# Moving the probabilities-times-V product to the end of each attention window in a two-layer transformer kernel

## Chip, core and metric

One core of a Trainium2 chip runs the whole kernel. The metric is the device time in microseconds (us). Five engines work side by side, each through its own list of instructions in order: TensorE (PE in the rows; PEld is its weight load), VectorE (DVE), ScalarE (ACT), GpSimd (POOL) and SyncE (SP, which here only issues DMAs). They meet through semaphores.

## What is computed

Two transformer layers on 2 x 512 tokens of width 256, all in float32. The part that matters here is the second attention, with 16 heads of width 128, causal:

```python
x = x + L0_attn(layernorm(x))      # 3 heads of width 256
x = x + L0_ffn(layernorm(x))       # ternary weights, 256 -> 1024 -> 256
# second attention, on layernorm(x):
q = x @ W_Q + b_Q;  k = x @ W_K + b_K;  v = x @ W_V + b_V     # 16 heads
scores = where(causal, q @ k.T / sqrt(128), -100000)
z = softmax(scores) @ v
x = x + z @ W_O + b_O
x = x + int8_linear(layernorm(x))
```

## The kernel before

Every matmul in higher precision is done three times, on operands split into a high and a low part (`split_mm`, lines 266 to 270: high times high, and the two mixed products). So each result of a matmul is read twice from its PSUM bank: ACT writes the rounded part (`..._hi`), and then DVE writes what is left (`..._lo`).

The first layer's attention is folded: a matrix GF = Wq.T Wk for each of 3 heads (uses 0 to 2 of the loop at lines 322 to 337) and Wv.T fcT (uses 3 to 5). The loads for it are issued by SP (lines 278 to 291) and ACT (lines 622 to 627). The first layer norm stands in the middle of this loop on PE (`layernorm_turn(0)` before use 2, line 326) and its vector part ahead of all on DVE (line 955).

The second attention runs in 32 windows, w = 4p + ww: p is the pair of heads (8 pairs, whose weights are loaded together into the tile `stage`), and the four windows of a pair are 2 batches x 2 heads. The last windows overlap the next pair: the loop runs `window(p, ww)` for ww = 1 to 4, after a single `window(0, 0)`. Each engine goes through a window by an order written out by hand (lines 211 to 222), with one letter and a number for each step:

- T0 to T3: the normalised probabilities PR of token block 0 to 3 of this window are transposed on PE (`turn`, 10 transposes in all), split by ACT (PT_hi, `probs_hi`) and DVE (PT_lo, `probs_lo`).
- A0: probabilities times V on PE (`attend`, 12 matmuls); on ACT and DVE A0 is the split of its result Z (`z_high`, `z_low`).
- O0, O1: Z times W_O on PE (`project_out`), and on DVE its sum into X (`add_out`). They stand in even windows alone. O0 in the window ww = 2 needs the Z of the window before it.
- S0 to S3: scores of the **next** window on PE (`scores`), the masked maximum on DVE (`max1`), the exponential on ACT (`exp1`). S3 on PE must not start before DVE has taken the maximum of S1, since both use bank 3 (line 501).
- Q0, K1, V2: projections for the window after the next, split by ACT and DVE. W2 on ACT and DVE is the split of the V2 that PE ended the window before with.
- B0 is, in the two last windows, the split of the Z of the window before.

`recip1` on DVE inverts the sums of the exponentials (part 0 for blocks 0 to 2, part 1 for block 3), POOL then multiplies PR by them (`normalise`), and T0 to T3 of the next window wait for that (line 512). Per pair, `load_a` (parts 0, 1, 2 for the weights of Q, K, V, on DVE) and `split_a` (POOL) split the new weights in windows ww = 1 and 2, `load_b` and `split_b` those of W_O in ww = 4.

## Time and profile before

| | |
|---|---|
| time of the kernel, median of 3 runs | 552.83 us (551.98 to 553.96) |
| the profiled execution's own time | 551.98 us |
| its span in the trace | 550.1 us |
| PE busy | 523.9 us, 95% of the span |
| DVE, ACT, POOL busy | 71%, 50%, 35% |
| one pair in the steady state (four windows) | 43.35 us |

The span is the stretch that the trace covers; 1.9 us of the time lie around it. Rows of a timeline are: start in us from the span's start, duration in us, engine, line of the kernel, operation, output tile <- input tiles, partitions x elements, number of instructions merged into the row, and in square brackets the idle time before it with what ended it. Durations of instructions that follow each other on an engine overlap a little (by 0.05 to 0.1 us), so what one costs its engine is the distance of the starts. Times on PE are distances of starts too, since its ends are modelled. Rows of a table of stretches give the stretch and its length, then the busy us and number of instructions of PE, PEld, DVE, ACT and POOL, the granted clock of PE as a share of 2.4 GHz, the DMA share and GB/s.

### The profile page before, as it was taken

How to read it: one execution, taken by the hardware profiler on the slowest of the kernel's cores; microseconds unless marked ns; L12 is line 12 of the kernel's file. 1: busy time of each engine (PE TensorE's matmuls, PEld its weight loads, DVE VectorE, ACT ScalarE, POOL GpSimd, SP SyncE). 2: the span in 40 equal slices, each digit the busy share in tenths (PEclk: the TensorE clock that was granted, in tenths of full speed). 3: DMA queues.
4: the chain of work that ended last, by engine and by line, in shares of the span. 5: the costliest groups of instructions: out<-in, count | busy, mean ns of one | idle time of the engine just before them, and what ended most of it. 6: DMA issues, size and time to landing. Idle time of an engine off the chain costs nothing.

```text
span 550.1 us, 9165 instructions
## 1 busy us (share of the span) xinstructions
PE 523.9 (95%) x3280; PEld 465.2 (85%) x3280; DVE 393.0 (71%) x992; ACT 277.5 (50%) x671; POOL 191.3 (35%) x274
## 2 busy tenths in 40 slices
...
GB/s 269 352 1 1 1 1 1 2 0 1 2 1 1 1 78 1 1 78 1 1 78 1 1 38 42 1 1 78 1 2 78 1 1 77 2 1 0 2 0 77
DMA packets 8316, 17.52 MB, mean 32 GB/s; under 512 B 464, under 2 KB 6736, under 8 KB 7248
## 3 DMA queue, kind: packets, MB, share of 16 engines
...
q8 instruction: 27, 0.44, 0.3%
...
HBM read 15.88 MB, written 1.05 MB: 31 GB/s over the span
## 4 chain that ended last, share of the span: by engine, by line
PE 67%; DVE 15%; ACT 8%; issue 5%; DMA 2%; POOL 1%; SPq 0%; DVEq 0%; ACTq 0%
PE bank L268 16%; PE bank L270 16%; PE bank L269 16%; ACT PR L721 5%; PE bank L515 4%; DVE SM L1212 3%; PE bank L442 3%; PE bank L441 3%; DMA fcT_sb<-fcT 2%; PE bank L507 2%; PE bank L505 2%; PE bank L506 2%; ACT K_hi L716 2%; PE bank L452 1%; PE bank L454 1%
## 5 line engine op out<-in xcount | busy, mean ns | idle before, releaser
L721 ACT ACTIVATE PR<-SM,nmax 128x128 f32<-128x128 f32 (+3 forms) x128 | 71.8, 562 | 120.1 <-DVE nmax L1212 120.1
L870 POOL TENSOR_TENSOR PR<-PR,rec 128x128 f32<-128x128 f32 x32 | 12.8, 400 | 151.0 <-DVE rec L1219 151.0
L1212 DVE CUSTOM_DVE_ANT_0 SM<-bank,causal 128x128 f32<-128x128 f32 (+3 forms) x128 | 60.2, 480 | 0.0
L1223 DVE TENSOR_TENSOR PT_lo<-bank,PT_hi 128x128 fp32r<-128x128 f32 (+3 forms) x128 | 59.5, 487 | 0.5 <-ACT PT_hi L726 0.3
L832 POOL TENSOR_TENSOR E_lo<-E,E_hi 128x512 fp32r<-128x512 f32 x24 | 31.1, 1301 | 57.7 <-DVE E_hi L1024 50.7
L515 PE MATMUL bank<-ident,PR 128*128 128x128 f32 x320 | 48.1, 276 | 3.2 <-POOL PR L879 1.1
L268 PE MATMUL bank<-XT_hi,W_hi 128*128 128x512 f32 x128 | 50.6, 396 | 0.1
L270 PE MATMUL bank<-XT_hi,W_lo 128*128 128x512 f32 x128 | 50.6, 395 | 0.0
L269 PE MATMUL bank<-XT_lo,W_hi 128*128 128x512 f32 x128 | 50.5, 394 | 0.0
L726 ACT CAST PT_hi<-bank 128x128 fp32r<-128x128 f32 (+3 forms) x128 | 48.6, 420 | 1.2 <-PE bank L515 1.0
L505 PE MATMUL bank<-K_hi,Q_hi 128*128 128x256 f32 (+2 forms) x128 | 46.6, 364 | 0.0
L268 PE MATMUL bank<-PT_hi,V_hi 128*128 128x256 f32 (+2 forms) x128 | 43.4, 339 | 1.4 <-DVE PT_lo L1223 1.4
L515 PEld LDWEIGHTS bank<-ident,PR 128*128 128x128 f32 x320 | 36.3, 140 | 9.8 <-POOL PR L879 3.6
L1202 DVE SCALAR_TENSOR_TENSOR Q_lo<-bank,bqk,Q_hi 128x512 fp32r<-128x512 f32 x32 | 24.0, 750 | 28.4 <-ACT Q_hi L716 28.4
L270 PE MATMUL bank<-PT_hi,V_lo 128*128 128x256 f32 (+2 forms) x128 | 42.2, 330 | 0.0
L269 PE MATMUL bank<-PT_lo,V_hi 128*128 128x256 f32 (+2 forms) x128 | 42.1, 329 | 0.0
L507 PE MATMUL bank<-K_hi,Q_lo 128*128 128x256 f32 (+2 forms) x128 | 41.6, 325 | 0.0
L506 PE MATMUL bank<-K_lo,Q_hi 128*128 128x256 f32 (+2 forms) x128 | 41.4, 324 | 0.0
L655 ACT ACTIVATE E<-bank,nmax 128x512 f32<-128x512 f32 x24 | 16.5, 689 | 48.8 <-DVE nmax L1018 48.8
L268 PE MATMUL bank<-WO_hi,Z_hi 128*128 128x256 f32 x128 | 36.7, 287 | 1.8 <-DVE Z_lo L1229 1.8
L1229 DVE SCALAR_TENSOR_TENSOR Z_lo<-bank,bv,Z_hi 128x512 fp32r<-128x512 f32 x32 | 23.9, 747 | 18.6 <-ACT Z_hi L731 17.9
L1219 DVE RECIPROCAL rec<-sum 128x3 f32<-128x3 f32 x64 | 10.7, 168 | 36.7 <-ACT PR L721 36.7
...
## 6 DMA issues: line engine op xcount, KB each, us to landing
...
wraw<-wgateT SPq DMA_DIRECT2D x1, 1024.0 KB, 12.8
...
```

Of the source, the lines that this page charges most:

```text
L268: pe.matmul(dst, a_hi, b_hi, start=first, stop=False, skip_group_check=share)
L269: pe.matmul(dst, a_hi, b_lo, start=False, stop=False, skip_group_check=share)
L270: return pe.matmul(dst, a_lo, b_hi, start=False, stop=last, skip_group_check=share)
L505: pe.matmul(dst[:, 0:n], Q_hi[:, slot, cols], K_hi[:, slot, 0:n], start=True, stop=False)
L506: pe.matmul(dst[:, 0:n], Q_hi[:, slot, cols], K_lo[:, slot, 0:n], start=False, stop=False)
L507: pe.matmul(dst[:, 0:n], Q_lo[:, slot, cols], K_hi[:, slot, 0:n], start=False, stop=True).then_inc(s_psum, 1)
L515: mm = pe.transpose(bank[4 + c % 2][:, j * P:(j + 1) * P], PR[:, c, j * P:(j + 1) * P], ident[:])
L721: act.activation(PR[:, c, 0:(c + 1) * P], SM[:, c % 2, 0:(c + 1) * P], ACT.Exp, bias=nmax1[:, c:c + 1], scale=-1.0, accum_out=sum1[:, c:c ...
L726: act.copy(PT_hi[:, 0:c + 1, c * P:(c + 1) * P], bank[4 + c % 2][:, 0:(c + 1) * P].rearrange("p (j q) -> p j q", q=P)).then_inc(pt_hi, 1)
L832: pool.tensor_tensor(E0_lo[:, m, :], E0[:, m, :], E0_hi[:, m, :], ALU.subtract).then_inc(e0_lo, 1)
L1212: dve.tensor_tensor_reduce(SM[:, c % 2, 0:n], bank[2 + c % 2][:, 0:n], causal[:, SEQ - n:SEQ], 1.0, HIGHEST, ALU.add, ALU.min, nmax1[:, c: ...
L1223: dve.tensor_tensor(PT_lo[:, 0:c + 1, c * P:(c + 1) * P], bank[4 + c % 2][:, 0:(c + 1) * P].rearrange("p (j q) -> p j q", q=P), PT_hi[:, 0 ...
```

## The change

**Orders of the windows.** On PE, A0 moves from the middle to the very end of each window, and Q0 stands in third place in even windows too. On ACT and DVE the split of Z is taken out of the window and stands as B0 in the next one: first of all on ACT, and on DVE behind T1 and ahead of S0. The split of V2 moves the other way, from the next window (W2) into its own (V2). `recip1` gets a letter of its own (R0, R1), R1 behind V2. On DVE `load_a` part 0 moves ahead of S2, part 1 to the end of window 1, part 2 to the start of window 2. POOL's `split_a`, `split_b` move to fit.

```diff
-        EVEN_PE = steps("T0 T1 S0 O0 T2 T3 S1 Q0 S2 O1 A0 K1 S3 V2")
-        EVEN_ACT = steps("T0 T1 W2 O0 S0 T2 T3 S1 Q0 S2 O1 A0 K1 S3")
-        EVEN_DVE = steps("T0 T1 S0 W2 O0 T2 T3 S1 Q0 S2 O1 A0 K1 S3")
-        ODD_PE = steps("T0 T1 S0 Q0 T2 T3 S1 S2 K1 A0 S3 V2")
-        ODD_ACT = steps("T0 T1 W2 S0 Q0 T2 T3 S1 S2 K1 A0 S3")
-        ODD_DVE = steps("T0 T1 S0 W2 Q0 T2 T3 S1 S2 K1 A0 S3")
+        EVEN_PE = steps("T0 T1 S0 Q0 O0 T2 T3 S1 S2 K1 O1 S3 V2 A0")
+        EVEN_ACT = steps("B0 T0 T1 W2 S0 Q0 T2 T3 S1 S2 K1 S3 V2")
+        EVEN_DVE = steps("T0 T1 B0 S0 W2 Q0 O0 T2 T3 S1 S2 K1 R0 O1 S3 V2 R1")
+        ODD_PE = steps("T0 T1 S0 Q0 T2 T3 S1 S2 K1 S3 V2 A0")
+        ODD_ACT = steps("B0 T0 T1 S0 Q0 T2 T3 S1 S2 K1 S3 V2")
+        ODD_DVE = steps("T0 T1 B0 S0 Q0 T2 T3 S1 S2 K1 R0 S3 V2 R1")
-        LAST = {"pe": (steps("T0 T1 S0 S1 O0 T2 T3 S2 O1 S3 A0"), steps("T0 T1 T2 T3 A0")),
-                "act": (steps("T0 T1 W2 S0 S1 T2 T3 S2 S3"), steps("T0 T1 T2 T3 B0 A0")),
-                "dve": (steps("T0 T1 S0 S1 W2 O0 T2 T3 S2 O1 S3"), steps("T0 T1 T2 T3 B0 A0"))}
+        LAST = {"pe": (steps("T0 T1 S0 S1 T2 T3 O0 S2 S3 O1 A0"), steps("T0 T1 T2 T3 A0")),
+                "act": (steps("B0 T0 T1 S0 S1 T2 T3 S2 S3"), steps("B0 T0 T1 T2 T3 A0")),
+                "dve": (steps("T0 T1 B0 S0 S1 T2 T3 O0 S2 R0 S3 O1 R1"), steps("T0 T1 B0 T2 T3 A0"))}
...
-                if first and kind == "O":
+                if first and kind in "OB" or kind == "W" and not first:
...
             def window(p, ww, first=False, last=False):
                 w = 4 * p + ww
+                if ww == 2 and not last:
+                    dve.wait_ge(pj_lo, 12 * p + 12)
+                    load_a(p + 1, 2)
...
-                        if c == CT - 2 and ww == 1 and not last:
+                        if c == 1 and ww == 1 and not last:
                             dve.wait_ge(pj_lo, 12 * p + 10)
                             load_a(p + 1, 0)
...
+                if ww == 1 and not last:
+                    dve.wait_ge(pj_lo, 12 * p + 11)
+                    load_a(p + 1, 1)
```

**Start.** The loads are issued in the order Wk (3), X of batch 0, Wv by head (3, was one), X of batch 1, the three biases, the int8 weights; fcT goes to ACT's queue. Eight matmuls on a tile of ones run on PE before the first load has landed. The first layer norm moves behind uses 3 and 4 on PE, and into the loop on DVE; the vector part of the second one (`ln_normalise(1)`) moves behind the first split of Y.

```diff
+            for _ in range(WARM):
+                pe.matmul(bank[0][:, 0:P], ones[:], ones[:], start=True, stop=True)
             for g in range(GF_USES):
                 h = g % H0
-                pe.wait_ge(*((ld_qk0[h], 32) if g < H0 else (ld_v0, 32)))
-                if g == 2:
+                if g < H0:
+                    pe.wait_ge(ld_qk0[h], 32)
+                else:
+                    pe.wait_ge(ld_v0[h], 16)
+                    pe.wait_ge(ld_fc, 16)
+                if g == H0 + 2:
+                    pe.wait_ge(consts, 1)
                     layernorm_turn(0)
...
             y_low(0)
+            ln_normalise(1)
```

On PE, in an odd window, from the first row of K1 (the projection of K, twice three matmuls) on. Before, `PT_hi,V_hi` (A0) stands between K1 and the last scores:

```order
L268 MATMUL bank<-XT_hi,W_hi 128x512 [waits pj_lo]
...
L270 MATMUL bank<-XT_hi,W_lo 128x512
L268 MATMUL bank<-PT_hi,V_hi 128x512 [waits z_free,t_free]
L269 MATMUL bank<-PT_lo,V_hi 128x512
...
L505 MATMUL bank<-K_hi,Q_hi 128x512 [waits s_max]
L506 MATMUL bank<-K_lo,Q_hi 128x512
```

The changed kernel at the same place, where S3 (`K_hi,Q_hi` of 512 columns, which waits for a maximum) is next to K1, and A0 follows V2 (`W_hi,XT_hi`):

```order
L271 MATMUL bank<-XT_hi,W_hi 128x512 [waits pj_lo]
...
L273 MATMUL bank<-XT_hi,W_lo 128x512
L518 MATMUL bank<-K_hi,Q_hi 128x512 [waits s_max]
L519 MATMUL bank<-K_lo,Q_hi 128x512
L520 MATMUL bank<-K_hi,Q_lo 128x512
L271 MATMUL bank<-W_hi,XT_hi 128x256 [waits pj_lo]
...
L271 MATMUL bank<-PT_hi,V_hi 128x512 [waits z_free,t_free]
```

So the last scores come one A0 earlier behind K1. On DVE, the end of window ww = 1 and the start of ww = 2. Before (`W_hi<-stage` is `load_a`, `SM,nmax` is `max1`):

```order
L1139 CAST W_hi<-stage 128x512 [waits pj_lo]
L1140 COPY bqk<-stage 128x2
L1229 SCALAR_TENSOR_TENSOR Z_lo<-bank,bv,Z_hi 128x512 [waits z_hi]
L1212 ISA SM,nmax<-bank,causal 128x512 [waits s_exp,s_psum,masks]
L1212 ISA nmax 128x1
L1219 RECIPROCAL rec<-sum 128x1 [waits s_exp]
L1223 TENSOR_TENSOR PT_lo<-bank,PT_hi 128x128 [waits pt_hi]
L1223 TENSOR_TENSOR PT_lo<-bank,PT_hi 128x2x128 [waits pt_hi]
L1212 ISA SM,nmax<-bank,causal 128x128 [waits s_exp,s_psum,masks]
```

The changed kernel on DVE at the same place:

```order
L1219 ISA SM,nmax<-bank,causal 128x512 [waits s_exp,s_psum,masks]
L1219 ISA nmax 128x1
L1206 TENSOR_TENSOR V_lo<-bank,V_hi 128x512 [waits pj_hi]
L1226 RECIPROCAL rec<-sum 128x1 [waits s_exp]
L1146 CAST W_hi<-stage 128x512 [waits pj_lo]
L1147 COPY bqk<-stage 128x2
L1149 CAST W_hi<-stage 128x512 [waits pj_lo]
L1230 TENSOR_TENSOR PT_lo<-bank,PT_hi 128x128 [waits pt_hi]
L1230 TENSOR_TENSOR PT_lo<-bank,PT_hi 128x2x128 [waits pt_hi]
L1236 SCALAR_TENSOR_TENSOR Z_lo<-bank,bv,Z_hi 128x512 [waits z_hi]
L1219 ISA SM,nmax<-bank,causal 128x128 [waits s_exp,s_psum,masks]
```

Between the last maximum and the first PT_lo there now stand V_lo and two loads of weights, and Z_lo has come between PT_lo and the first maximum of the window.

## Rows read from the trace of the kernel before

**Rows 1.** Page, its head: the span and busy time of each engine.

```profile
span 550.1 us, 9165 instructions
PE 523.9 (95%) x3280; PEld 465.2 (85%) x3280; DVE 393.0 (71%) x992; ACT 277.5 (50%) x671; POOL 191.3 (35%) x274
```

**Rows 2.** Windows ww = 1 to 4: stretch, length, then busy us and instructions.

```profile
241.32:250.58 9.26, 9.26 (x61) 8.26 (x59) 7.59 (x23) 6.12 (x16) 2.76 (x6) 1.00 0.34 114
250.58:263.26 12.68, 12.48 (x84) 11.25 (x83) 8.73 (x23) 6.45 (x16) 4.58 (x7) 1.00 0.00 0
263.26:272.58 9.32, 9.32 (x60) 8.23 (x59) 6.64 (x19) 6.12 (x16) 2.39 (x5) 1.00 0.01 2
272.58:284.67 12.09, 12.09 (x85) 11.26 (x84) 8.13 (x23) 6.51 (x16) 3.64 (x6) 1.00 0.01 1
```

**Rows 3.** Timeline, PE, window ww = 3: its T0, T2, A0 and S3.

```profile
263.26 0.49 PE L515 MATMUL bank<-ident,PR 128*128 128x128 f32 x3
...
265.36 0.94 PE L515 MATMUL bank<-ident,PR 128*128 128x128 f32 x7
...
268.43 0.50 PE L268 MATMUL bank<-PT_hi,V_hi 128*128 128x512 f32 x1
...
270.46 0.39 PE L505 MATMUL bank<-K_hi,Q_hi 128*128 128x512 f32 x1
```

**Rows 4.** Timeline, DVE, the same window: T0 and T1, S0, Q0, T2 and T3, S1, A0.

```profile
264.52 0.70 DVE L1223 TENSOR_TENSOR PT_lo<-bank,PT_hi 128x128 fp32r<-128x128 f32 x2
265.14 0.28 DVE L1212 CUSTOM_DVE_ANT_0 SM<-bank,causal 128x128 f32<-128x128 f32 x1
...
266.57 0.75 DVE L1202 SCALAR_TENSOR_TENSOR Q_lo<-bank,bqk,Q_hi 128x512 fp32r<-128x512 f32 x1 [0.53 <-ACT Q_hi L716]
267.23 1.14 DVE L1223 TENSOR_TENSOR PT_lo<-bank,PT_hi 128x384 fp32r<-128x384 f32 x2
268.30 0.41 DVE L1212 CUSTOM_DVE_ANT_0 SM<-bank,causal 128x256 f32<-128x256 f32 x1
...
271.39 0.75 DVE L1229 SCALAR_TENSOR_TENSOR Z_lo<-bank,bv,Z_hi 128x512 fp32r<-128x512 f32 x1
272.05 0.68 DVE L1212 CUSTOM_DVE_ANT_0 SM<-bank,causal 128x512 f32<-128x512 f32 x1
```

**Rows 5.** Timeline, ACT: Z of one window, then S3, T0 and T1, Q0.

```profile
259.94 0.69 ACT L731 ACTIVATE Z_hi<-bank,bv 128x512 fp32r<-128x512 f32 x1 [0.41 <-PE bank L270]
...
263.53 0.72 ACT L721 ACTIVATE PR<-SM,nmax 128x512 f32<-128x512 f32 x1 [1.43 <-DVE nmax L1212]
...
264.25 0.52 ACT L726 CAST PT_hi<-bank 128x128 fp32r<-128x128 f32 x2
...
265.86 0.67 ACT L716 ACTIVATE Q_hi<-bank,bqk 128x512 fp32r<-128x512 f32 x1
```

**Rows 6.** Timeline, DVE, the last step of window ww = 1.

```profile
252.33 0.17 DVE L1219 RECIPROCAL rec<-sum 128x1 f32<-128x1 f32 x1 [0.88 <-ACT PR L721]
```

**Rows 7.** Timeline, DVE, window ww = 1: the splits of the new weights.

```profile
247.10 0.42 DVE L1134 TENSOR_SCALAR W_hi<-stage 128x512 fp32r<-128x512 f32 x1
...
247.56 0.69 DVE L1137 SCALAR_TENSOR_TENSOR W_lo<-stage,W_hi 128x512 fp32r<-128x512 f32 x1
...
249.34 0.78 DVE L1139 CAST W_hi<-stage 128x512 fp32r<-128x512 f32 x1
```

**Rows 8.** Timeline of the start: GF uses 0 and 1, uses 3 to 5, second layer norm.

```profile
4.91 6.56 PE L336 MATMUL bank<-Wk_sb,Wq_sb 128*128 128x256 f32 x16 [4.91 <-DMA Wk_sb<-wk]
...
15.87 5.45 PE L336 MATMUL bank<-fcT_sb,Wv_sb 128*128 128x256 f32 x24 [1.79 <-DMA fcT_sb<-fcT]
...
20.93 3.07 DVE L939 TENSOR_SCALAR XN<-X,ln_mv,ln_rs 128x256 f32<-128x256 f32 x4
```

**Rows 9.** Windows near the end; the last three numbers are PEclk, DMA share, GB/s.

```profile
519.00:522.40 3.40, 1.37 (x9) 0.87 (x9) 2.92 (x11) 2.12 (x5) 0.96 (x2) 1.00 0.00 0
522.40:525.80 3.40, 3.40 (x12) 3.04 (x12) 2.30 (x8) 0.00 (x0) 1.52 (x2) 0.50 0.00 0
```

More of the change, by code:

```diff
@@ L33 @@
 H0 = 3
+WARM = 8
 DE = 1024
@@ L160, in build @@
         ld_qk0 = [sem(f"ld_qk0_{h}") for h in range(H0)]
-        ld_v0, ld_bias, ld_qw = sem("ld_v0"), sem("ld_bias"), sem("ld_qw")
+        ld_v0 = [sem(f"ld_v0_{h}") for h in range(H0)]
+        ld_fc, ld_bias, ld_qw = sem("ld_fc"), sem("ld_bias"), sem("ld_qw")
+        warm_set = sem("warm_set")
         ld_w = [sem(f"ld_w{i}") for i in range(3)]
@@ L280, in _ @@
                              wk0[h].rearrange("(k p) e -> p k e", p=P)).then_inc(ld_qk0[h], 16)
-                if h == 0:
-                    sp.dma_start(X[:, 0:CT, :], x[0].rearrange("(c p) d -> p c d", p=P)).then_inc(ld_x[0], 16)
-            sp.dma_start(Wv_sb[:], wv0.rearrange("h (k p) e -> p (h k) e", p=P)).then_inc(ld_v0, 16)
-            sp.dma_start(fcT_sb[:], fcT.rearrange("(k p) o -> p k o", p=P)).then_inc(ld_v0, 16)
+            sp.dma_start(X[:, 0:CT, :], x[0].rearrange("(c p) d -> p c d", p=P)).then_inc(ld_x[0], 16)
+            for h in range(H0):
+                sp.dma_start(Wv_sb[:, KD * h:KD * (h + 1), :],
+                             wv0[h].rearrange("(k p) e -> p k e", p=P)).then_inc(ld_v0[h], 16)
             sp.dma_start(X[:, CT:TILES, :], x[1].rearrange("(c p) d -> p c d", p=P)).then_inc(ld_x[1], 16)
+            for dst, row in ((fcb_bc, fcb), (bo_bc, bo1), (qb_bc, qb)):
+                sp.dma_start(dst[:], row.rearrange("(a d) -> a d", a=1).to_broadcast([P, D])).then_inc(ld_bias, 16)
+            sp.dma_start(qw_sb[:], qw.rearrange("(k p) d -> p k d", p=P)).then_inc(ld_qw, 16)
             for i, w in enumerate((wupT, wgateT)):
@@ L624, in _ @@
                               wq0[h].rearrange("(k p) e -> p k e", p=P)).then_inc(ld_qk0[h], 16)
-            act.dma_start(qw_sb[:], qw.rearrange("(k p) d -> p k d", p=P)).then_inc(ld_qw, 16)
-            for dst, row in ((fcb_bc, fcb), (bo_bc, bo1), (qb_bc, qb)):
-                act.dma_start(dst[:], row.rearrange("(a d) -> a d", a=1).to_broadcast([P, D])).then_inc(ld_bias, 16)
+            act.dma_start(fcT_sb[:], fcT.rearrange("(k p) o -> p k o", p=P)).then_inc(ld_fc, 16)
             def layernorm_hi(k):
@@ L759, in window @@
                         project_hi(w + 2, ww + 2, c)
+                    elif kind == "V":
+                        project_hi(w + 2, ww + 2, c)
                     elif kind == "W":
-                        if first:
-                            layernorm_hi(5)
+                        layernorm_hi(5)
                         project_hi(w + 1, ww + 1, c)
@@ L884, in window @@
                 if not (last and ww == 3):
-                    normalise(w + 1, 0)
+                    if ww == 2 and not last:
+                        split_a(p + 1, 2)
                     if ww == 4:
                         split_b(p + 1)
+                    normalise(w + 1, 0)
+                    normalise(w + 1, 1)
                     if ww == 1 and not last:
                         split_a(p + 1, 1)
-                    normalise(w + 1, 1)
                     if last and ww == 2:
                         rstd(6)
-                    if ww == 1 and not last:
-                        split_a(p + 1, 2)
             rstd(5)
@@ L994, in _ @@
                                          ALU.mult, ALU.subtract).then_inc(pj0_done, 1)
[L995 removed]
+                if g == H0 - 2:
+                    dve.wait_ge(ld_x[0], 16)
+                    ln_statistics(0)
+                    ln_variance(0)
+                if g == H0 - 1:
+                    ln_normalise(0)
+                if g == H0 + 1:
                     layernorm_lo(0)
[L997 removed]
                     dve.wait_ge(ld_x[1], 16)
                     ln_statistics(1)
[L1000 removed]
+                if g == H0 + 2:
                     ln_variance(1)
[L1002 to L1003 removed]
             acts = [GF_USES]
@@ L1256, in window @@
                 w = 4 * p + ww
+                if ww == 2 and not last:
+                    dve.wait_ge(pj_lo, 12 * p + 12)
+                    load_a(p + 1, 2)
                 for kind, c in window_work("dve", ww, first, last):
@@ L1259, in window @@
                         probs_lo(w, c)
+                        if last and ww == 3 and c == 1:
+                            dve.wait_ge(o_free, 4 * PAIRS - 1)
+                            ln_statistics(6, 2, CT)
+                        if last and ww == 3 and c == CT - 1:
+                            ln_variance(6)
                     elif kind == "S":
```

60 lines of the change are left out of this document (16 added, 44 removed).

## Prediction

> **What bounds the kernel now.** Read the head of the page first [rows 1]: PE is busy for 523.9 of 550.1 us. A change of order can give back only what PE idles, or make it idle more. Next the table of stretches for one pair of heads in the steady state [rows 2]: its four windows take 9.26, 12.68, 9.32 and 12.09 us, 43.35 in all. The two even ones do the same work on PE, so 12.68 holds 0.59 us of waiting, and the odd one of 9.32 some 0.1. That makes 0.7 us of idle PE in a pair, and seven such pairs give 4.9 us: all that the middle of the kernel has to give. The start has more: PE waits 4.9 us for the first loads and 1.8 us for fcT [rows 8]. Then comes the timeline of one odd window on PE, DVE and ACT [rows 3 to 5], which shows how close DVE runs behind PE. DVE is busy for 71% of the span only [rows 1], but it works through its list in order, and what counts is when its maximum of S1 is ready.
>
> **The new orders, odd window.** Count from the first transpose, 263.26 [rows 3]. K1 ends on PE where A0 starts, at 268.43, or 5.17 us in. S3 starts 2.03 us later, at 7.20, and A0 is what lies between. The change takes A0 away from there, so PE wants to start S3 at 5.17. S3 waits for DVE's maximum of S1. In the trace of before that one starts at 268.30 and takes 0.41 [rows 4]: it is ready at 5.45, hidden under A0 so far, and by itself already 0.3 us too late for the new place.
>
> It also comes later than that. The new list on ACT begins with the split of Z, which can start when the product at the end of the last window is through: ACT starts it 0.2 us after PE's last issue (it waited for nothing but PE in the row of 259.94 [rows 5]). It keeps ACT for 0.6, so the first PT_hi starts at 0.8 and the first PT_lo 0.27 later (264.25 and 264.52 [rows 4, 5]), at 1.07. Two PT_lo take 0.62 (264.52 to 265.14 [rows 4]), then Z_lo takes 0.66 (271.39 to 272.05 [rows 4]), and only then comes the maximum of S0, at 2.35. Before, it stood at 265.14, or 1.88. From there on the steps have the distances of the rows: Q_hi 0.72 after that maximum (265.14 to 265.86), Q_lo 0.71 after Q_hi, PT_lo of T2 and T3 0.66 after that, and the maximum of S1 1.07 after those [rows 4, 5]. That is 2.35 + 0.72 + 0.71 + 0.66 + 1.07 = 5.51, and ready at 5.92. PE starts S3 at about 6.0 and **waits 0.85 us in each odd window**.
>
> **Even window.** PE comes to O0 after T0, T1, S0 and Q0, which take 2.10 (263.26 to 265.36 [rows 3]). If DVE and ACT are up to date, Z_lo starts at 1.69 and is done at 2.44: a wait of 0.4. They aren't. In the odd window before, the maximum of S1 starts at 5.51; then follow S2's maximum (some 0.5, between S1's 0.41 and S3's 0.68 [rows 4]), the exponentials of S1 and S2 on ACT (1.1 between them), K_hi and K_lo, so that the maximum of S3 comes at about 8.6 (in the rows at 272.05, or 8.79 [rows 4]: no gain here, though PE has the scores 1 us earlier). S3's exponential starts 0.72 after it and takes 0.72 (263.53 to 264.25 [rows 5]), then V_hi and V_lo at 0.6 each (the sizes of Z_hi and Z_lo less their overlap [rows 4, 5]) and the reciprocal at 0.15 (0.17 [rows 6]) follow, which now stand in this window: DVE ends its list at 11.4, while PE ended its own at 9.24 + 0.85 = 10.1. So DVE starts the even window 1.3 us late, its first PT_lo is 0.27 later than in a clean one, and O0 starts at 2.8: **a wait of 0.7** (price 12.09 + 0.7 = 12.8). The even window's own slack (O0 and O1 are 2.87 us of PE work, 12.09 less 9.22) lets DVE catch up before it ends.
>
> **Windows ww = 1 and 2, with new weights.** Part 0 of `load_a` takes 1.07 us (247.10 to 248.17, 0.46 + 0.61 by its first and last start [rows 7]) and now stands ahead of S2's maximum, so everything after is 1.05 us later: DVE reaches the end of V_lo and the reciprocal at 12.45. Then come part 1 with 0.76 (0.78 in its row [rows 7]) and part 2 with 0.33 (a copy like the first 0.42 of part 0, less the overlap), both ahead of the first PT_lo: 13.54. PE has ended its list at 10.1. The first transposes wait 0.1 and 0.4 us for POOL, whose reciprocal is late by the same 1.05. PT_lo starts 3.4 us into window ww = 2, Z_lo ends 1.36 after that, and O0 starts at 15.0 on the clock of window ww = 1, where PE could have had it at 12.7: **waits of 2.3 and 0.5**. Before, the same end of the list cost 0.6 us: DVE stood 0.88 for the reciprocal with a ready PT_lo behind it [rows 6]. That wait goes, as do the 0.7 us of a pair.
>
> **Sum for a pair:** 0.85 (ww = 3) + 0.7 (ww = 4) + 0.85 (ww = 1) + 2.8 (ww = 2) - 0.7 = +4.5 us, a pair of 47.9 us. Seven pairs: **+31.5 us**. DMAs of the weights are issued by SP after `split_b`, which keeps its place, about 1 us before the pair ends: no change.
>
> **First window and end.** In window 0 the layer norm's split comes first, and Q0 now stands ahead of T2, T3 and S1, which had filled that wait: 1.1 us of PE work (transposes 0.68, scores 0.44) lie bare, and DVE's arrears make 0.7 more: +1.8. The bounds are 0 (Q0 not waiting) and 3. In the last pair: an odd window's 0.85, then a short even one (S0 and S1 early, no projections) in which T3 waits for POOL behind R1, and O1 for DVE's sum: +1.5, and 0.6 where Z_lo and statistics stand ahead of T2's PT_lo: **+3.0**, bounds 1 and 5.
>
> **Start.** Wv and fcT were one load of 768 KB and one of 256, and PE waited for them until 15.87 [rows 8]. Now use 3 needs head 0 of Wv and fcT alone, 2.5 MB in all instead of 3.6, at the rate of the loads some 3 us earlier (about 12); use 2 ends at about 12.5. Uses 3 to 5 take 5.2 us (24 matmuls at 0.22 [rows 8]) and the layer norm 1.0, so the projections of Y start at 18.8 where they did at 20.96: 2.1. Behind them DVE's normalisation of 3.07 us stood ahead of a GF_lo that PE waited for [rows 8]; it moves behind Y_lo: 0.9 back. **-3.0 us**, bounds 0 and -4.5. The eight warming matmuls cost nothing, PE idles there. In the rows the first uses run at 0.43 us a matmul up to 10.4 and at 0.22 after, the two levels of 1.2 and 2.4 GHz. The Trainium skill ("TensorE: Matmul & The Clock Gate", section "What's actually happening") says that the low clock is the default and activity releases it. By that rule the warming could bring the clock forward, and the start would give up to 4.1 and the time be 584; by the rows it stays open, since nothing runs between the warming and 4.9.
>
> **Total:** 551.98 (the profiled execution's own time, 0.85 under the median of the runs shown) - 3.0 + 1.8 + 31.5 + 3.0 = **585.3 us**.
>
> **Rivals.**
> *Weights off the path.* If ACT and DVE make up in window ww = 2 what the loads cost (the chain over exponentials and K_lo has gaps that the loads may fill), windows ww = 1 and 2 are like 3 and 4: 2 x 1.55 - 0.7 = +2.4 a pair, +17 in all, **571**. For it: DVE is busy for 7.59 of 9.26 us in ww = 1 [rows 2], so some room is left. Against: part 1 and 2 stand bare between two lists.
> *Short waits.* The 0.3 us that the rows show for S3 and 0.4 for O0: 1.4 - 0.7 = +0.7 a pair, **558**.
> *The other side: faster.* If the maximum of S1 is ready before 5.17 us into an odd window and Z_lo before 2.1 us into an even one, nothing replaces the 0.7 us that go. Both ACT and DVE would have to be 0.8 us faster between the transposes and S1. Then 551.98 - 3.0 - 4.9 = **544**. It decides at S3: in the rows the maximum is at 5.45 even without Z_lo ahead of it.
> *The clock falls.* Near the end PE was busy for 1.37 of 3.40 us and then stood at 0.50 [rows 9], 1.2 GHz. The wait of 2.3 us in ww = 2 is about as bare. If the clock falls behind it, some 1.7 us of PE's work are lost each time; seven times is 12: **597**. Against: 0.4 and 2.3 us of waiting have 1.9 us of work between them.
> *It doesn't do what it says.* If the start is bound by the rate of the loads alone, -3.0 becomes 0: 588, inside the range.
>
> **Chances.** Forecast 0.65 (575 to 595), weights off the path 0.13, short waits 0.05, faster 0.05, clock 0.12. The range takes the forecast, most of the first rival and of the clock: **566 to 599**. Within 0.3% of before, about what a measurement of this kernel can tell from no change: 0.02, from the cases between short waits and faster; faster 0.04; slower 0.94.
>
> **What would show it.** After the change: the last scores of each odd window wait for DVE's maximum of S1 by 0.85 us; O0's first matmul waits for Z_lo by 0.7 us in ww = 4 and over 2 in ww = 2; a pair takes 47.9 us; DVE has no idle time between `load_a` part 1 and Z_lo; PE's busy time is unchanged, its share falls to about 90%. The projections of Y start near 18.8. The forecast is wrong if a pair takes under 45 us, or if PEclk falls in the middle of the kernel.

## The result, and the profile after

| | before | after |
|---|---|---|
| time, median | 552.86 us (551.98 to 553.96, 4 runs) | 586.95 us (585.75 to 589.03, 4 runs) |
| ratio to before, 95% interval | | 1.062 (1.0584 to 1.0655) |
| the profiled execution, its span | 551.98 us, 550.1 us | 585.75 us, 584.0 us |
| one pair in the steady state | 43.35 us | 47.8 us |

The kernel is 6.2% slower; 585.3 was forecast. The head of the page answers to [rows 1]: PE's busy time rose by 6.6 us, 3.8 of them the warming matmuls (the forecast had it unchanged), and 27.3 us more of the span are idle PE.

```profile
span 584.0 us, 9198 instructions
...
PE 530.5 (91%) x3296; PEld 466.9 (80%) x3296; DVE 389.9 (67%) x992; ACT 274.4 (47%) x671; POOL 193.4 (33%) x274
```

The view of waits says who PE waits for (in total, times, longest). The wait for a maximum (nmax) has 15 entries, one for each odd window but the last. Of the 15 for Z_lo, 14 are the even windows of the seven pairs; the last, of 1.8 us in the final window, stood in the kernel before too.

```profile
PE bank L271 <- DVE Z_lo L1236: 18.7, 15, 1.9
PE bank L518 <- DVE nmax L1219: 11.0, 15, 0.9
...
PE bank L271 <- DVE XT_lo L959: 2.4, 2, 2.1
```

The table of stretches for one pair, ww = 4, 1, 2, 3 in that order, answers to [rows 2]:

```profile
328.92:341.74 12.82, 12.29 (x85) 11.18 (x84) 8.43 (x23) 6.56 (x17) 3.16 (x6) 1.00 0.01 3
341.74:352.00 10.26, 9.50 (x61) 8.20 (x59) 7.09 (x21) 4.93 (x13) 1.92 (x5) 1.00 0.30 103
352.00:366.57 14.57, 12.54 (x83) 11.25 (x83) 9.24 (x27) 7.47 (x19) 6.17 (x9) 1.00 0.01 2
366.57:376.72 10.15, 9.46 (x61) 8.24 (x59) 5.67 (x17) 5.75 (x16) 2.39 (x5) 1.00 0.00 0
```

| window | before | forecast | after |
|---|---|---|---|
| ww = 1 | 9.26 | 10.1 | 10.26 |
| ww = 2 | 12.68 | 14.9 | 14.57 |
| ww = 3 | 9.32 | 10.1 | 10.15 |
| ww = 4 | 12.09 | 12.8 | 12.82 |

On PE's timeline the waits stand where the forecast put them. The first rows are from ww = 4 (O0), then S3 and the start of A0 in ww = 1, the first transposes of ww = 2 and its O0, and S3 of ww = 3, which answers to [rows 3]:

```profile
331.69 0.36 PE L271 MATMUL bank<-WO_hi,Z_hi 128*128 128x256 f32 x1 [0.53 <-DVE Z_lo L1236]
...
347.78 0.50 PE L518 MATMUL bank<-K_hi,Q_hi 128*128 128x512 f32 x1 [0.76 <-DVE nmax L1219]
...
350.00 0.39 PE L271 MATMUL bank<-PT_hi,V_hi 128*128 128x512 f32 x1
...
352.00 0.90 PE L528 MATMUL bank<-ident,PR 128*128 128x128 f32 x3
...
356.53 0.36 PE L271 MATMUL bank<-WO_hi,Z_hi 128*128 128x256 f32 x1 [1.89 <-DVE Z_lo L1236]
...
372.55 0.50 PE L518 MATMUL bank<-K_hi,Q_hi 128*128 128x512 f32 x1 [0.69 <-DVE nmax L1219]
```

DVE's timeline from the maximum of S1 in ww = 1 to Z_lo in ww = 2 answers to [rows 4, 6, 7]:

```profile
347.31 0.41 DVE L1219 CUSTOM_DVE_ANT_0 SM<-bank,causal 128x256 f32<-128x256 f32 x1
...
347.64 0.42 DVE L1141 TENSOR_SCALAR W_hi<-stage 128x512 fp32r<-128x512 f32 x1
...
350.62 0.75 DVE L1209 SCALAR_TENSOR_TENSOR K_lo<-bank,bqk,K_hi 128x512 fp32r<-128x512 f32 x1 [1.35 <-ACT K_hi L727]
...
351.37 0.66 DVE L1219 CUSTOM_DVE_ANT_0 SM<-bank,causal 128x512 f32<-128x512 f32 x1
...
353.39 0.69 DVE L1206 TENSOR_TENSOR V_lo<-bank,V_hi 128x512 fp32r<-128x512 f32 x1 [1.35 <-ACT V_hi L724]
354.00 0.15 DVE L1226 RECIPROCAL rec<-sum 128x1 f32<-128x1 f32 x1
354.07 0.41 DVE L1146 CAST W_hi<-stage 128x512 fp32r<-128x512 f32 x1
354.39 0.37 DVE L1147 COPY bqk<-stage 128x2 f32<-128x2 f32 x1
354.67 0.41 DVE L1149 CAST W_hi<-stage 128x512 fp32r<-128x512 f32 x1
355.01 0.61 DVE L1230 TENSOR_TENSOR PT_lo<-bank,PT_hi 128x128 fp32r<-128x128 f32 x2
355.54 0.73 DVE L1236 SCALAR_TENSOR_TENSOR Z_lo<-bank,bv,Z_hi 128x512 fp32r<-128x512 f32 x1
```

From 353.39 on DVE has no idle time until Z_lo is done, while PE waits. Before that it stood still twice for 1.35 us: the same list holds a pause and, just behind it, a jam.

Where the 33.9 us of the two spans went (lengths between first transposes):

| stretch | before | after | difference | forecast |
|---|---|---|---|---|
| start, to the first T0 | 186.97 | 184.77 | -2.2 | -3.0 |
| window 0 | 10.78 | 13.50 | +2.7 | +1.8 |
| seven pairs | 303.68 | 334.63 | +30.95 | +31.5 |
| last ww = 1 and 2 | 17.13 | 19.64 | +2.5 | +3.0 with the tail |
| tail | 31.54 | 31.42 | -0.1 | |

### The profile page after: what moved, and what is told of

Read it like the earlier page. It is cut to its first block, busy times and chain, and to the rows that moved or that the text cites. A ratio compares the mean times of both kernels' runs of the same rounds, so it can differ in the third digit from the quotient of the medians.

```text
span 584.0 us, 9198 instructions
## 1 busy us (share of the span) xinstructions
PE 530.5 (91%) x3296; PEld 466.9 (80%) x3296; DVE 389.9 (67%) x992; ACT 274.4 (47%) x671; POOL 193.4 (33%) x274
## 4 chain that ended last, share of the span: by engine, by line
PE 52%; DVE 26%; ACT 13%; issue 6%; DMA 1%; POOL 0%; DVEq 0%; ACTq 0%
PE bank L271 13%; PE bank L273 12%; PE bank L272 12%; ACT PR L732 6%; DVE PT_lo L1230 5%; DVE Z_lo L1236 4%; DVE SM L1219 4%; PE bank L455 3%; PE bank L454 3%; PE bank L528 2%; DVE Q_lo L1209 2%; ACT Z_hi L742 2%; DVE V_lo L1206 2%; ACT K_hi L727 2%; ACT Q_hi L727 1%
## 5 line engine op out<-in xcount | busy, mean ns | idle before, releaser
L882 POOL TENSOR_TENSOR PR<-PR,rec 128x128 f32<-128x128 f32 x32 | 12.8, 402 | 164.7 <-DVE rec L1226 164.7
L518 PE MATMUL bank<-K_hi,Q_hi 128*128 128x256 f32 (+2 forms) x128 | 48.4, 378 | 11.0 <-DVE nmax L1219 11.0
L737 ACT CAST PT_hi<-bank 128x128 fp32r<-128x128 f32 (+3 forms) x128 | 48.8, 428 | 14.9 <-PE bank L528 14.9
L271 PE MATMUL bank<-WO_hi,Z_hi 128*128 128x256 f32 x128 | 38.1, 298 | 19.0 <-DVE Z_lo L1236 18.7
L1209 DVE SCALAR_TENSOR_TENSOR K_lo<-bank,bqk,K_hi 128x512 fp32r<-128x512 f32 x32 | 24.0, 751 | 42.4 <-ACT K_hi L727 42.4
L1206 DVE TENSOR_TENSOR V_lo<-bank,V_hi 128x512 fp32r<-128x512 f32 x32 | 22.1, 691 | 40.7 <-ACT V_hi L724 40.7
L271 PEld LDWEIGHTS bank<-WO_hi,Z_hi 128*128 128x128 f32 x128 | 24.8, 194 | 25.9 <-issue 24.5
L528 PEld LDWEIGHTS bank<-ident,PR 128*128 128x128 f32 x320 | 37.6, 142 | 8.7 <-POOL PR L885 2.6
L271 PE MATMUL bank<-PT_hi,V_hi 128*128 128x256 f32 (+2 forms) x128 | 41.3, 323 | 1.7 <-DVE PT_lo L1230 1.7
```

Of the source, the lines that this page charges most:

```text
L271: pe.matmul(dst, a_hi, b_hi, start=first, stop=False, skip_group_check=share)
L518: pe.matmul(dst[:, 0:n], Q_hi[:, slot, cols], K_hi[:, slot, 0:n], start=True, stop=False)
L528: mm = pe.transpose(bank[4 + c % 2][:, j * P:(j + 1) * P], PR[:, c, j * P:(j + 1) * P], ident[:])
L737: act.copy(PT_hi[:, 0:c + 1, c * P:(c + 1) * P], bank[4 + c % 2][:, 0:(c + 1) * P].rearrange("p (j q) -> p j q", q=P)).then_inc(pt_hi, 1)
L1209: ins = dve.scalar_tensor_tensor(lo[:, ww % 2, :], src, bqk[:, 2 * which + h:2 * which + h + 1], hi[:, ww % 2, :], ALU.add, ALU.subtract)
```

## Experiments

"L518" below is S3 on PE, "Z_lo" what O0 waits for. Where a kernel ran once ("one run"), its one time is given, with no interval; differences of some 1 us are then read from its window lengths and not from its time. The kernel before ran beside each. The diffs show the lines that tell, with `...` where others are left out; the same move is made in the lists of the other windows where they hold the step.

**1. The start alone.** The kernel before with the loads, the warming matmuls and the layer norms of the changed one; its windows are untouched.

```diff
         EVEN_PE = steps("T0 T1 S0 O0 T2 T3 S1 Q0 S2 O1 A0 K1 S3 V2")
...
+            for _ in range(WARM):
+                pe.matmul(bank[0][:, 0:P], ones[:], ones[:], start=True, stop=True)
...
+            ln_normalise(1)
```

> The kernel before with the new start alone: order of the loads, eight warming matmuls, first layer norm behind uses 3 and 4, second normalisation behind Y_lo. Theory (the start gives 2.2 us at the first transpose of the second attention, 186.97 before and 184.77 after, and the windows give nothing): 552.9 - 2.2 = 550.7 us, a pair stays at 43.35 us. Rival (the start's gain is swallowed in the first attention window, where PE waits for POOL and DVE): 552.9, no difference.

Measured: 548.11 us, ratio 0.9907 (0.9885 to 0.9928), which is below both forecasts. The first T0 is at 183.74 us, 3.2 before that of the kernel before; a pair takes 43.35 us as ever, and the tail 30.76 us instead of 31.54. That makes 3.9 us between the two profiled executions. The medians lie 5.4 apart; the execution of the kernel before that was profiled was its fastest, and where the others spend the rest isn't shown. On the changed kernel's timeline of PE, the start answers to [rows 8]:

```profile
0.98 3.78 PE L329 MATMUL bank<-ones 128*128 128x128 f32 x16 [0.98 <-POOL ones L811]
4.97 5.45 PE L349 MATMUL bank<-Wk_sb,Wq_sb 128*128 128x256 f32 x24 [0.21 <-DMA Wk_sb<-wk]
...
17.06 0.50 PE L271 MATMUL bank<-XT_hi,GF_hi 128*128 128x512 f32 x1 [0.27 <-DVE XT_lo L959]
```

The warming ends 0.21 us ahead of the first load, and the first 24 matmuls take 5.45 us, 0.227 each, where the first 16 took 6.56 us before [rows 8], or 0.41 each. Uses 0 to 2 are so at the level of 2.4 GHz from the first one. Use 3 starts right behind them, at 10.47, and waits for no load. The projections of Y start at 17.06 us (18.8 forecast, 20.96 before).

**2. The windows alone.** The other half, with the start of the kernel before.

```diff
...
-        ODD_PE = steps("T0 T1 S0 Q0 T2 T3 S1 S2 K1 A0 S3 V2")
+        ODD_PE = steps("T0 T1 S0 Q0 T2 T3 S1 S2 K1 S3 V2 A0")
...
```

> The kernel before with the new orders of the windows alone, and the old start. Theory (start and windows are independent): 586.95 + 2.2 = 589.2 us, a pair at 47.8 us, the clock as in the changed kernel. Rival (part of the loss in the windows comes from the new start, by the phase of clock or DMA): under 586 us.

Measured: 591.35 us, ratio 1.0676 (1.0645 to 1.0708), a pair of 47.8 us. The forecast of 589.2 was too low because it had the start at 2.2 us. So the halves add: 591.35 less the 5.4 us of the start is 586.0, against 586.95. One thing more: in the profiled execution ww = 2 of the first pair took 16.13 us instead of 14.57. In the table of stretches its first 4.7 us are at full clock with PE busy for 2.67, and the next 3.4 at half:

```profile
213.01:217.70 4.69, 2.67 (x14) 1.90 (x14) 3.13 (x12) 2.47 (x7) 3.41 (x5) 1.00 0.00 0
217.70:221.10 3.40, 3.40 (x17) 3.40 (x18) 1.44 (x2) 0.99 (x4) 1.32 (x2) 0.50 0.02 5
```

That is the rival "the clock falls", once instead of seven times, for 1.56 us. It stands behind the same wait of 1.9 us at O0 that the other pairs have without a fall.

**3. S3 behind V2 in odd windows.** This takes the wait of S3 away on PE and nothing on DVE.

```diff
-        ODD_PE = steps("T0 T1 S0 Q0 T2 T3 S1 S2 K1 S3 V2 A0")
+        ODD_PE = steps("T0 T1 S0 Q0 T2 T3 S1 S2 K1 V2 S3 A0")
```

> The changed kernel with one swap, on PE and in odd windows alone: V2 ahead of S3, so that PE has 1.42 us of work while it would wait for the maximum of S1. Theory A (the list of DVE and ACT is the path from one window into the next, and the wait of S3 hides a part of it): the wait of 0.9 us at S3 goes, but comes back at O0 of the following even window (0.7 becomes 1.5, 2.05 becomes 2.9), and a pair stays at 47.8 us, the kernel at 585 to 587. Theory B (the waits are separate prices, as the prediction adds them): a pair loses 1.8 us and is 46.0, the kernel about 573.

Measured: 588.54 us (one run), a pair of 47.76 us. The time is higher because the clock was low for 6.8 us in window 0, which took 14.74 us, and once in ww = 2 of the first pair, which took 16.15. The row of L518 is gone from the waits, ww = 3 takes 9.17 us, and ww = 4, whose own lists are untouched, 13.76 instead of 12.82:

```profile
PE bank L271 <- DVE Z_lo L1236: 22.7, 15, 1.9
PE bank L528 <- POOL PR L882: 7.2, 8, 1.0
```

```profile
368.48:377.65 9.17, 9.17 (x61) 8.32 (x59) 5.65 (x17) 4.82 (x13) 1.45 (x4) 1.00 0.00 0
377.65:391.41 13.76, 12.52 (x84) 11.21 (x83) 8.43 (x25) 7.46 (x19) 4.07 (x8) 1.00 0.00 1
```

The 1.0 us of ww = 3 came back whole in the next window, most of it at O0, which waits 1.12 us instead of 0.53. In ww = 1, which still takes 10.26 us, the wait only moved: PE then stands 0.92 us for POOL ahead of the first transposes of ww = 2. PE's waits are where it meets a chain on ACT, DVE and POOL that runs through both windows. This step of PE, moved about, did not shorten that chain.

**4. The weights in DVE's pause.** Parts 1 and 2 of `load_a` go behind the maximum of S3 in ww = 1, where DVE stands for V_hi, which ACT makes behind the exponential of S3 (the 1.35 us at 353.39).

```diff
-                if ww == 1 and not last:
-                    dve.wait_ge(pj_lo, 12 * p + 11)
-                    load_a(p + 1, 1)
...
+                        if c == CT - 1 and ww == 1 and not last:
+                            dve.wait_ge(pj_lo, 12 * p + 11)
+                            load_a(p + 1, 1)
+                            dve.wait_ge(pj_psum, 12 * p + 12)
+                            load_a(p + 1, 2)
```

> The changed kernel with parts 1 and 2 of the weights' splits on DVE moved from behind the reciprocal R1 to directly behind the maximum of S3 in window ww = 1, where DVE then stands idle 1.35 us for V_hi. Theory (they stand bare between two lists): O0 in ww = 2 waits 1.0 instead of 2.05 us, a pair is 46.7 to 46.8 us, the kernel 579 us. Rival (PT_lo waits for ACT anyway, the loads cost nothing where they are): 47.8 and 586.

Measured: 578.22 us (one run), ww = 2 at 13.80 instead of 14.57. The waits for Z_lo fell from 18.7 to 11.5 us; in return transposes wait for POOL:

```profile
PE bank L271 <- DVE Z_lo L1236: 11.5, 15, 1.8
...
PE bank L528 <- POOL PR L885: 2.6, 7, 0.4
```

All seven pairs together take 5.0 of the 7.5 us between the two profiled executions: seven times 0.77 less 0.4 that ww = 1 of the first pair took more. The rest is window 0, which in this execution had no low clock (12.10 us against 13.50), and the first T0 at 183.74 against 184.77.

**5. Z_lo behind the maximum of S0.** The forecast had counted 0.66 us of Z_lo ahead of S0's maximum, and so ahead of S1's.

```diff
...
-        ODD_DVE = steps("T0 T1 B0 S0 Q0 T2 T3 S1 S2 K1 R0 S3 V2 R1")
+        ODD_DVE = steps("T0 T1 S0 B0 Q0 T2 T3 S1 S2 K1 R0 S3 V2 R1")
```

> The changed kernel with Z_lo on DVE behind the maximum of S0 instead of ahead of it, in all windows. Theory (Z_lo's 0.66 us stand in the chain to the maximum of S1): S3 in odd windows waits 0.3 instead of 0.9 us, O0 waits 0.2 us longer in even windows, a pair is 46.9 to 47.0 us, the kernel 580 to 581. Rival, from s3_behind_v2 (what S3 no longer waits, O0 waits more, since DVE's list is the path): a pair at 47.8 or above, the kernel 586 to 588.

Measured: 581.5 us (one run). The waits of S3 fell from 11.0 to 0.5 us and ww = 1 and 3 took 9.6 and 9.49 us; ww = 2 and 4 took 0.2 more each, since Z_lo is later there. A pair takes 46.9 us, 0.87 less, or 6.1 us in seven. But in three of the seven pairs ww = 2 took 16.35 instead of 14.8, which takes 4.7 us back. So the seven pairs are only 1.0 us shorter than in the changed kernel, and most of the drop in time is window 0, which again had no low clock (12.09 us), and the start. What speaks for the theory is the pair and not the time. In the table of stretches, one of them up to where its clock fell and the 3.4 us from there, and one of the others whole:

```profile
299.98:304.90 4.92, 2.69 (x14) 1.91 (x14) 3.14 (x12) 3.36 (x9) 3.64 (x6) 0.99 0.00 0
304.90:308.30 3.40, 3.40 (x17) 3.40 (x17) 1.44 (x2) 0.12 (x2) 1.09 (x1) 0.51 0.00 0
348.42:363.22 14.80, 12.59 (x84) 11.27 (x84) 9.37 (x27) 7.46 (x19) 6.16 (x9) 1.00 0.01 2
```

The wait at O0 there is 2.10 us, 0.2 longer than in the changed kernel, whose pairs showed no fall.

**6. V split in the next window again.** ACT and DVE get V2's split out of the end of the list.

```diff
...
-        ODD_ACT = steps("B0 T0 T1 S0 Q0 T2 T3 S1 S2 K1 S3 V2")
-        ODD_DVE = steps("T0 T1 B0 S0 Q0 T2 T3 S1 S2 K1 R0 S3 V2 R1")
+        ODD_ACT = steps("B0 T0 T1 W2 S0 Q0 T2 T3 S1 S2 K1 S3")
+        ODD_DVE = steps("T0 T1 B0 S0 W2 Q0 T2 T3 S1 S2 K1 R0 S3 R1")
...
```

> The changed kernel with the split of V2 on ACT and DVE back in the next window (behind T1 on ACT, behind the maximum of S0 on DVE), so that the list of a window ends with S3 and R1. Theory (DVE stands idle 1.35 us for V_hi at the end of every list and then carries 0.6 us of V_lo, all ahead of the next window's PT_lo and Z_lo): O0 waits 0.45 instead of 0.7 in ww = 4 and 0.9 instead of 2.05 in ww = 2, a pair is 46.3 to 46.5, the kernel 576. Rival (ACT's Z_hi behind the end of A0 is what the next window waits for): 47.8 and 586.

Measured: 577.41 us (one run), a pair of 46.65 us (10.25, 13.52, 10.13, 12.73): 1.15 less, all but 0.1 of it in ww = 2. The waits for Z_lo are 10.7 us instead of 18.7, those of S3 11.2 as before.

**7. Three repairs together.** Experiments 4, 5 and 6 in one kernel, with A0 still last on PE.

```diff
...
-        ODD_DVE = steps("T0 T1 B0 S0 Q0 T2 T3 S1 S2 K1 R0 S3 V2 R1")
+        ODD_DVE = steps("T0 T1 S0 B0 W2 Q0 T2 T3 S1 S2 K1 R0 S3 R1")
...
+                            load_a(p + 1, 1)
+                            dve.wait_ge(pj_psum, 12 * p + 12)
+                            load_a(p + 1, 2)
```

> The changed kernel, A0 still last on PE, with three repairs of DVE's list together: maximum of S0 ahead of Z_lo, V split in the next window, weights of K and V loaded in the pause behind the maximum of S3. One at a time they took 0.9, 1.15 and 0.75 us off a pair of 47.8. Theory that each took away work of its own from one chain: they add, the pair is 45.0 us, the time 566 to 569. Rival: they overlap, since each only fills the same pause of DVE behind the maximum of S3; then the pair stays above 46 and the time above 573.

Measured: 569.6 us (one run), a pair of 45.6 us: 2.2 of the 47.8, where the three alone had given 0.87, 1.15 and 0.75. The first forecast (45.0) is the nearer one, but they don't add in full. The 0.6 us missing are in ww = 2, which takes 13.5 as in experiment 6: once V is gone from there, the loads in the pause give at most the 0.2 us that the later Z_lo cost in experiment 5. These edits show the source of half of the 4.45 us that a pair had grown by. The other half is left, and is read from the waits alone, those for Z_lo at O0 and for POOL:

```profile
PE bank L271 <- DVE Z_lo L1237: 10.6, 15, 1.8
...
PE bank L528 <- POOL PR L886: 2.6, 7, 0.4
```

**8. A0 in the middle again, the other lists as changed.**

```diff
-        EVEN_PE = steps("T0 T1 S0 Q0 O0 T2 T3 S1 S2 K1 O1 S3 V2 A0")
+        EVEN_PE = steps("T0 T1 S0 Q0 O0 T2 T3 S1 S2 O1 A0 K1 S3 V2")
-        ODD_PE = steps("T0 T1 S0 Q0 T2 T3 S1 S2 K1 S3 V2 A0")
+        ODD_PE = steps("T0 T1 S0 Q0 T2 T3 S1 S2 K1 A0 S3 V2")
```

> The changed kernel with the product of probabilities and V back in the middle of each window on PE (ahead of K1's row in even windows, behind it in odd ones); everything on DVE, ACT and POOL stays as in the changed kernel, so Z is still split in the next window and V in its own. Theory: the place of A0 accounts only for the waits of S3 (0.7 + 0.8 us in a pair, gone now); the rest of the loss comes from what DVE has to do between the end of one window and Z_lo (V_lo, reciprocal, loads of weights, PT_lo), which is unchanged. So odd windows near 9.4 us, even ones 12.7 and 14.2 to 14.6, a pair of 45.8 to 46.3, time 572 to 576 us. Rival: the late A0 is the whole cost, since it also makes Z late; then the pair is near 43.4 to 44 and the time 552 to 560.

**9. The same with V split in the next window** (experiment 6 added to it).

```diff
...
-        ODD_DVE = steps("T0 T1 B0 S0 Q0 T2 T3 S1 S2 K1 R0 S3 V2 R1")
+        ODD_DVE = steps("T0 T1 B0 S0 W2 Q0 T2 T3 S1 S2 K1 R0 S3 R1")
...
-        ODD_PE = steps("T0 T1 S0 Q0 T2 T3 S1 S2 K1 S3 V2 A0")
+        ODD_PE = steps("T0 T1 S0 Q0 T2 T3 S1 S2 K1 A0 S3 V2")
```

> The changed kernel with both of its moves on V and A0 undone: the product of probabilities and V in the middle of each window on PE, and V's split in the next window; Z is still split in the next window, Q0 still early. It is the fourth corner of a square: A0 late and V in its own window takes 47.8 us a pair, A0 late and V next 46.65, A0 in the middle and V in its own 52.2 (pair without a low clock). Theory, taken from the third corner: what costs is a split of V that ACT and DVE must make behind PE's last product, ahead of the next window's first transposes; a late A0 covers part of it and costs 1.4 us in a pair at S3. Then with V's split out of the way the middle place is the better one: odd windows 9.4, even ones 12.4 and 13.2, a pair of 44.0 to 44.8, time 559 to 564 us. Rival: A0 in the middle is bad by itself in these lists, since its Z waits for the next window anyway; then the pair stays above 46.6 and the time above 576.

Measured: 629.72 and 609.13 us (one run each), pairs of 52.2 to 54.6 and 50.1 to 51.2 us. Part of each range is the clock: the pairs of 52.2 and 50.1 had no fall. Both of my forecasts were far off, and so was the theory behind the second. The timeline of DVE in experiment 9, at the end of an even window, shows what I had overlooked:

```profile
474.70 0.75 DVE L1210 SCALAR_TENSOR_TENSOR K_lo<-bank,bqk,K_hi 128x512 fp32r<-128x512 f32 x1 [4.32 <-ACT K_hi L727]
475.37 0.17 DVE L1227 RECIPROCAL rec<-sum 128x3 f32<-128x3 f32 x1
475.45 0.66 DVE L1243 TENSOR_TENSOR X<-bank,X 128x512 f32<-128x512 f32 x1
476.03 0.68 DVE L1220 CUSTOM_DVE_ANT_0 SM<-bank,causal 128x512 f32<-128x512 f32 x1
...
477.60 0.16 DVE L1227 RECIPROCAL rec<-sum 128x1 f32<-128x1 f32 x1 [0.88 <-ACT PR L732]
```

The old order of PE has K1 behind A0, at 472.32 us here. DVE's new list has the reciprocal for the next T0 to T2 (R0) and the sum into X behind K_lo; in the kernel before both stood ahead of it. So DVE stood 4.32 us for K_hi with those two steps queued behind it. In ww = 4 the cast for the split of W_O (`load_b`) stands behind K_lo as well, and POOL's `split_b` ahead of its normalisation: the first transposes of ww = 1 then wait 2.2 us for POOL, and PE waits for POOL 16.6 us in all. These runs don't price A0's place: they price lists that don't fit each other. That the misfit is the whole of it is read from the timelines and was not tried by an edit. What the late A0 costs with lists made for it is not settled. It is at most the 45.6 of experiment 7 less the 42.75 of experiment 10, 2.9 us a pair, with the new place of Z's split in it.

**10. The good halves: new start, one load in the pause.** The start of experiment 1, the windows of the kernel before, and part 1 of `load_a` behind the maximum of S3, with POOL's `split_a` behind its second normalisation.

```diff
...
+                        if c == CT - 1 and ww == 1 and not last:
+                            dve.wait_ge(pj_lo, 12 * p + 11)
+                            load_a(p + 1, 1)
...
-                        if kind == "K" and ww == 1 and not last:
-                            dve.wait_ge(pj_lo, 12 * p + 11)
-                            load_a(p + 1, 1)
```

> start_only (the old orders with the new start, 548.1 us) with one more edit, in window ww = 1: on DVE part 1 of the weights' split moves from behind K_lo to behind the maximum of S3, and POOL's split_a of part 1 moves behind the second normalise. Theory (in ww = 2 PE waits 0.6 us for T2 and T3 since S3's maximum came 0.76 us late): windows ww = 2 take 12.1 instead of 12.7, a pair 42.75 instead of 43.35, the kernel 548.1 - 4.2 = 544 us. Rival (another wait of the same size stands behind it): 548.

Measured: **543.16 us** (543.03 to 543.28), ratio 0.9814 (0.9781 to 0.9847): faster than both kernels, than the one before by 1.9%. A pair takes 42.76 us instead of 43.35. That is 4.3 us in the seven pairs of the two traces, of the 4.9 us to experiment 1; most of the rest is the tail (30.08 against 30.76 us). DVE's load and POOL's `split_a` were moved together and not tried one by one. DVE's pause behind the maximum of S3 was 0.88 us [rows 6]; the load now lies in it, 0.47 us of it are left, and ww = 2 takes 12.08 us, all of it busy on PE, instead of 12.68 [rows 2]. Two rows of DVE's timeline, and ww = 2 in the table of stretches:

```profile
289.69 0.42 DVE L1145 CAST W_hi<-stage 128x512 fp32r<-128x512 f32 x1
...
290.66 0.17 DVE L1225 RECIPROCAL rec<-sum 128x1 f32<-128x1 f32 x1 [0.47 <-ACT PR L732]
```

```profile
289.62:301.70 12.08, 12.08 (x85) 11.26 (x83) 9.21 (x24) 6.39 (x16) 4.93 (x7) 1.00 0.01 2
```

**11. Q0 early on top of it.** Only the third place of Q0 in even windows is taken over from the change, on PE, ACT and DVE.

```diff
-        EVEN_PE = steps("T0 T1 S0 O0 T2 T3 S1 Q0 S2 O1 A0 K1 S3 V2")
+        EVEN_PE = steps("T0 T1 S0 Q0 O0 T2 T3 S1 S2 O1 A0 K1 S3 V2")
...
```

> start_gap with Q0 in third place in even windows, ahead of O0, on all three engines, as in the changed kernel; the rest of the old orders stays. Theory (an early Q0 costs nothing and covers the wait for T2): 543.5 to 544 us, a pair at 42.7. Rival (what is late in the changed kernel comes from the early Q0 too, which keeps ACT and DVE from T2 and T3): even windows over 12.3 us, the kernel above 546.

Measured: 547.15 us (545.62 to 548.9), ratio 0.9887 (0.9852 to 0.9923). The time is the rival's, the cause is neither's: the pairs take 42.76 us as in experiment 10, and window 0 takes 14.32 us instead of 10.79. On PE and in the table of stretches:

```profile
187.89 0.66 PE L271 MATMUL bank<-XT_hi,W_hi 128*128 128x512 f32 x1 [2.09 <-DVE XT_lo L958]
```

```profile
187.96:191.40 3.44, 3.44 (x11) 2.76 (x12) 0.42 (x1) 0.68 (x2) 1.48 (x3) 0.51 0.02 5
```

Q0 of window 0 waits 2.09 us for the layer norm's split, and the next 3.4 us run at half the clock.

**12. The same, with window 0 in its old order.**

```diff
...
-            order = ORDERS[engine][ww % 2]
+            order = FIRST[engine] if first else ORDERS[engine][ww % 2]
```

> The version with the new start, the loads of K's weights in the pause and Q0 early in even windows (547.15 us), but window 0 in the order of the kernel before. Theory: the early Q0 cost 3.5 us in window 0 alone, by a wait of 2.1 us for the split of the layer norm and the fall of the clock behind it, and nothing in the later windows, whose pairs take 42.8 us with it as without it. So window 0 takes 10.8 us and the time is 543 to 543.8 us. Rival: the later clock phases at the end are what cost (0.5 in the last 50 us); then 545 or more.

Measured: 544.77 us (543.78 to 545.96), ratio 0.9843 (0.981 to 0.9876). Window 0 takes 10.80 us again, as the theory said, but the time lies above its 543.8, and 1.6 us to experiment 10 remain, which ran on another chip. Between the profiled executions it is a start 0.7 us longer, and 1.7 in the tail, where the clock went up and down twice more. Both are at places that Q0's place doesn't touch; whether they belong to it stays open. In the pairs an early Q0 neither gains nor costs.

## Why the prediction was right, point by point

**The total: near, in part by luck.** 585.3 was forecast from the fastest execution of the kernel before, and the profiled one of the changed kernel took 585.75. By the table above the start and window 0 cost 0.8 and 0.9 us more than forecast, the seven pairs and the end 0.55 and 0.6 less. What carries the result is the pair: +4.5 forecast, +4.45 measured.

**Odd windows: right.** 5.51 and 6.0 were forecast for the start of S1's maximum and of S3. In ww = 1 they are 347.31 and 347.78, counted from 341.74: 5.57 and 6.04. Experiment 5 shows that Z_lo ahead of S0's maximum carries most of it: without it the waits of S3 are 0.5 us in all. Experiment 3 shows that this wait is a debt of DVE and not of PE: not paid at S3, it falls due in the next window.

**Even window ww = 4: right.** O0 starts 2.77 us into it (2.8 forecast) and the window takes 12.82. The wait before O0 is 0.53 us and not 0.7, since PE gets there at 2.24 and not at 2.1.

**Ww = 1 and 2, the weights: right in place, 0.3 us too dear.** DVE's reciprocal ends at 12.3 on the clock of ww = 1 (12.45 forecast), PT_lo starts at 13.27 (13.54) and O0 at 14.79 (15.0). The wait at O0 is 1.9 instead of 2.3, that at the transposes 0.13 instead of 0.5. The rival "weights off the path" fell in the changed kernel, and experiments 4 and 10 show how near it was: the room was there, in the 1.35 us in which DVE waits for ACT, one step ahead of where the loads stood.

**Window 0: too cheap by 0.9 us, and the step that failed is the clock.** 1.1 us of bare work and 0.7 of arrears were counted. The wait for XT_lo is 2.1 us, and behind it the granted clock was low from 189.1 to 192.5, for which the sum had no term; where it did not fall (experiments 4 and 5), window 0 took 12.1, or +1.3. By its words the forecast was to be wrong if PEclk fell in the middle of the kernel: it fell here, at a third of the span, and nowhere in the pairs that the sign was meant for.

**The start: the sum was right by two errors.** The projections of Y start 3.9 us earlier, not 2.1: uses 0 to 2 run at full clock and end at 10.4, where the sum had 12.5, and the first head of Wv and fcT have landed by then, where it had about 12. By the rule of the Trainium skill ("TensorE: Matmul & The Clock Gate", section "What's actually happening"), that activity releases a clock which is low by default, the start would give 4.1 and the time be 584. The trace agrees with the rule in the first matmuls (0.227 us each against 0.41) and, for the gain, as far as the first scores, 4.3 us earlier. But then a part is lost: `ln_normalise(1)`, moved behind Y_lo, stands on DVE ahead of the first maxima. I had counted its move as a gain of 0.9.

```profile
20.77 0.69 DVE L1018 TENSOR_TENSOR Y_lo<-bank,Y_hi 128x512 fp32r<-128x512 f32 x1 [0.70 <-ACT Y_hi L657]
21.38 2.54 DVE L951 TENSOR_SCALAR XN<-X,ln_mv,ln_rs 128x256 f32<-128x256 f32 x4
23.84 1.46 DVE L1024 TENSOR_REDUCE nmax<-bank 128x1 f32<-128x512 f32 x2
```

In the execution of experiment 1, 3.7 of 4.5 us are left at the second head's scores and 3.2 at the first T0. That the normalisation is the cause was not tried by itself, and there is a rival: in the same stretch the casts to E_hi take longer than in the kernel before (0.97 us at 25.27 in experiment 1, against 0.41 for the first one before). The profiled execution of the changed kernel lost one more us near 65 us, where an E_hi cast took 1.46. Those of experiments 6 and 8 lost as much at the same place, with casts of 1.49 and 1.56; those of 3, 4 and 5 did not.

**The end: +2.4 of the +3.0**, inside its bounds.

**The rival of the clock: it exists, but seldom.** Behind the wait of 1.9 us in ww = 2 the clock stayed up in all seven pairs of the changed kernel, and fell in one of seven each in experiments 2 and 3. One of 2.1 us (experiment 5) was followed by a fall in three pairs of seven, at 1.55 us each (1.7 had been estimated). So 586.95 lies near an edge: a fall in all seven pairs would cost, as an estimate from these 1.55 us, 11 us.

**Short waits** did not come: the pair grew by 4.45 us and not by 0.7 (its own terms give 558.7 us, not 558).

**The other side** would have needed ACT and DVE 0.8 us faster. Nothing in the change made them so: DVE's busy time is 389.9 against 393.0 us. The gain that PE could give was 4.9 us for all pairs, and one load moved by one step (experiment 10) took nearly all of it: 4.3 us.
